# Paged attention on one core: value pages gathered by POOL in four indirect transfers a sequence, in place of sixteen page loads from SP

## What is computed

```
q, k, v   = x Wq, x Wk, x Wv ; q, k normed and rotated        # 32 query heads, 8 key heads, 128 wide
kc, vc    = k_cache[block_table], v_cache[block_table]        # 16 pages of 32 rows: 512 cached keys a sequence
scores    = q . [kc, k] / sqrt(128) ; cached keys past cache_seqlens masked
o         = softmax(scores) @ [vc, v]
out       = x + o Wo
```

## Time and profile before

| | us |
|---|---|
| median of 3 runs | 2616.27 |
| lowest and highest of them | 2610.56, 2620.38 |
| the profiled execution's own time | 2625.55 |
| its span, first to last instruction | 2624.0 |
| PE busy | 2441.7 (93% of the span) |
| DVE busy | 1807.7 (69%) |
| ACT busy | 1592.3 (61%) |
| POOL busy | 428.6 (16%) |

### The profile page before, as it was taken

The page is one execution under the profiler, slowest core; times in us unless marked ns, Lnnn a source line. Parts: engine busy times, 40 slices in busy tenths (PEclk is TensorE's granted clock), DMA queues, the critical chain, the costliest instruction groups (busy, mean ns, idle before and its releaser), DMA issues. The chain is left out here.

```text
span 2624.0 us, 57577 instructions
## 1 busy us (share of the span) xinstructions
PE 2441.7 (93%) x16326; PEld 2210.3 (84%) x16327; DVE 1807.7 (69%) x3636; ACT 1592.3 (61%) x3277; POOL 428.6 (16%) x625
## 2 busy tenths in 40 slices
PE   6699799999999949999999999999999998599999
PEld 5578588877878839999999999999999998388887
DVE  5345336999999948887887778878777785544443
ACT  3122235777777848888888878878788785311111
POOL 1222231010001011222222222222222221000000
PEclk9899899999999979999999999999999999799999
DMA  6422342333333369999999999899999995756664
GB/s 220 148 74 75 124 140 84 97 103 99 100 94 92 89 192 257 294 283 285 290 281 291 282 286 279 276 290 281 279 289 279 275 292 148 275 204 216 219 216 152
DMA packets 388288, 541.09 MB, mean 206 GB/s; under 512 B 61667, under 2 KB 275363, under 8 KB 384356
## 3 DMA queue, kind: packets, MB, share of 16 engines
q1 hardware_dynamic: 352932, 450.10, 56.2%
q0 software_dynamic: 33152, 87.07, 10.2%
q10 hardware_dynamic: 2112, 2.89, 0.4%
HBM read 441.54 MB, written 98.30 MB: 206 GB/s over the span
## 5 line engine op out<-in xcount | busy, mean ns | idle before, releaser
L1514 PE MATMUL att_ps_o<-att_pt,att_v 128*128 128x128 f32 x4096 | 544.2, 276 | 23.0 <-DMA att_v<-in_v_pages 20.8
L1514 PEld LDWEIGHTS att_ps_o<-att_pt,att_v 128*128 128x128 f32 x4096 | 506.0, 192 | 28.5 <-issue 22.2
L1333 ACT ACTIVATE att_prob<-att_prob,att_shift 128x544 f32<-128x544 f32 x512 | 383.7, 749 | 210.0 <-DVE att_shift L1399 196.8
L76 PE MATMUL att_ps_s<-att_k_hi,att_q_hi 128*128 128x272 f32 x1024 | 339.3, 331 | 34.2 <-DVE att_k_lo L1430 22.4
L1399 DVE CUSTOM_DVE_ANT_0 att_prob<-att_ps_s,att_mask 128x544 f32<-128x544 f32 x512 | 366.5, 716 | 0.0
L1430 DVE TENSOR_TENSOR att_k_lo<-att_k_raw,att_k_hi 128x1024 fp32r<-128x1024 f32 (+1 forms) x320 | 338.5, 1058 | 19.6 <-ACT att_k_hi L1348 19.6
L76 PE MATMUL qkv_ps_y<-qkv_w_hi,qkv_xt_hi 128*128 128x512 f32 x768 | 316.2, 412 | 0.0
L1340 ACT ACTIVATE att_pt<-att_ps_pt 128x512 f32<-128x512 f32 x512 | 295.5, 577 | 31.9 <-PE att_ps_pt L1493 30.4
L1493 PE MATMUL att_ps_pt<-att_ident,att_prob 128*128 128x128 f32 x2048 | 309.5, 274 | 1.1 <-ACT att_pt L1340 1.1
L1348 ACT ACTIVATE att_k_hi<-att_k_raw 128x1024 fp32r<-128x1024 f32 (+1 forms) x320 | 292.8, 915 | 28.0 <-DMA att_k_raw<-in_k_pages 28.0
L78 PE MATMUL qkv_ps_y<-qkv_w_hi,qkv_xt_lo 128*128 128x512 f32 x768 | 302.6, 394 | 0.0
(11 more groups left out here) (178 smaller groups left out, 4688.1 us busy)
## 6 DMA issues: line engine op xcount, KB each, us to landing
att_k_raw<-in_k_pages SPq DMA_DIRECT2D x1024, 128.0 KB, 2.9
att_v<-in_v_pages SPq DMA_DIRECT2D x1024, 128.0 KB, 4.3
q_t<-qkv_out_t SPq DMA_DIRECT2D x128, 256.0 KB, 2.3
att_q_raw<-q_t POOLq DMA_DIRECT2D x64, 512.0 KB, 6.6
o_t<-att_o POOLq DMA_DIRECT2D x64, 512.0 KB, 7.4
out_o<-o_t SPq DMA_DIRECT2D x32, 1024.0 KB, 6.2
out_inv<-inv_t SPq DMA_DIRECT2D x32, 1024.0 KB, 6.5
qkv_w_stage<-in_w_qkv SPq DMA_DIRECT2D x12, 1024.0 KB, 5.2
```

Of the source, the lines that this page charges most:

```text
L76: pe.matmul(out, xh, wh, start=start, stop=False)
L1333: act.activation(prob[:, b, :], prob[:, b, :], ACT.Exp, bias=shift[:, b:b + 1], scale=-1.0, accum_out=total[:, j // HK, j % HK:j % HK + 1] ...
L1514: pe.matmul(out, v_sb[:, p, c, h * DH:(h + 1) * DH], pt_sb[:, j % OG, c, :], start=(c == 0), stop=False)
```

## The change

SP loads keys alone. POOL gathers the values: for each sequence four indirect transfers, each of 128 rows of 4 KB, one row into each of the 128 partitions, with row numbers read from SBUF, one a partition. DVE computes the row numbers of all sequences once at the start (`row_sb`: page number times 32 plus the row in the page, from the table, which is now loaded into all 128 partitions, 512 KB, and from `step`, an existing input). For each sequence POOL copies its four columns into `rows_now` between its first and second own-value transfer. POOL's iteration s now loads the own values and the values of s+1, and those of sequence 0 go ahead of the loop; queries and own keys of s+2 and the stores of s-2 stay in iteration s. SP and DVE wait for one count of four small loads; PE waits for 4 landings of values in place of 16. Two pairs of semaphores are merged.

```
-V_ORDER = [c * PPP + m for c in range(NPP // PPP) for m in (0, 2, 1, 3)]
...
+        table_sb, step_sb = m.sb("table", [P, NSEQ * NPP], i32), m.sb("step", [P, 1])
+        row_sb, rows_now = m.sb("row", [P, NSEQ * NPP // PPP], i32), m.sb("rows_now", [P, 2, NPP // PPP], i32)
...
-                def load_v(s, p, pages):
-
-                    if later(s, 2):
-                        sp.wait_ge(pv_done, HK * (s - 1))
-                    for n in V_ORDER:
-                        at = n % PPP * PSIZE
-                        sp.dma_start(v_sb[at:at + PSIZE, p, n // PPP, :], v_pages[bass.ds(pages[n], 1)])\
-                          .then_inc(v_loaded[p], 16)
...
+                sp.dma_start(table_sb[:, :], table).then_inc(small_loaded, 16)
+                sp.wait_ge(small_loaded, 64)
+                load_k(0, 0, pages_in(0))
                 load_k(1, 1, pages_in(1))
 
                 def pair(i, last):
 
                     if not last:
-                        next_pages = pages_in(2 * i + 2)
-                        load_k(2 * i + 2, 0, next_pages)
-                    load_v(2 * i + 1, 1, pages_in(2 * i + 1))
-                    if not last:
-                        load_k(2 * i + 3, 1, pages_in(2 * i + 3))
-                        load_v(2 * i + 2, 0, next_pages)
+                        for p in range(2):
+                            load_k(2 * i + 2 + p, p, pages_in(2 * i + 2 + p))
...
                     for u in range(OG):
+                        if u == 1:
+                            pool.tensor_copy(rows_now[:, p, :], row_sb[:, bass.ds(s * (NPP // PPP), NPP // PPP)])\
+                                .then_inc(rows_copied, 1)
+                            pool.wait_ge(rows_copied, s + 1)
                         pool.dma_start(vo_sb[u * SEQ:(u + 1) * SEQ, p, :, u, :], rows[:, :, u, :])\
                             .then_inc(own_v_loaded[p], 16)
+
+                def load_v(s, p):
+
+                    for c in range(NPP // PPP):
+                        pool.indirect_dma_start(
+                            v_sb[:, p, c, :], None, v_pages.rearrange("n k x -> (n k) x"),
+                            bass.IndirectOffsetOnAxis(ap=rows_now[:, p, c:c + 1], axis=0)).then_inc(v_loaded[p], 16)
...
+                pool.wait_ge(rows_ready, PPP + 2)
+                load_own_v(0, 0)
+                load_v(0, 0)
 
                 def pair(i, last):
+
+
                     for p in range(2):
                         s = 2 * i + p
-                        load_own_v(s, p)
+                        if not (last and p):
+                            load_own_v(s + 1, 1 - p)
+                            load_v(s + 1, 1 - p)
                         if not last:
                             load_q(s + 2, p)
                             load_own_k(s + 2, p)
...
+                row_f = prob[:, 0, 0:NSEQ * NPP // PPP]
+                for m_ in range(PPP):
+                    at = slice(m_ * PSIZE, (m_ + 1) * PSIZE)
+                    dve.tensor_copy(row_f[at, :], table_sb[at, :].rearrange("p (n m) -> p n m", m=PPP)[:, :, m_])\
+                       .then_inc(rows_ready, 1)
+                dve.wait_ge(rows_ready, PPP)
+                dve.tensor_scalar(row_f, row_f, float(PSIZE), step_sb[:, 0:1], ALU.mult, ALU.add).then_inc(rows_ready, 1)
+                dve.wait_ge(rows_ready, PPP + 1)
+                dve.tensor_copy(row_sb[:, :], row_f).then_inc(rows_ready, 1)
...
-                        pe.wait_ge(v_loaded[p], 16 * NPP * (i + 1))
+                        pe.wait_ge(v_loaded[p], 16 * (NPP // PPP) * (i + 1))
...
-        "table": a["itok_Bx16_0_63"].reshape(1, -1),
+        "table": everywhere(a["itok_Bx16_0_63"]),
```

More of the change, by code:

```diff
@@ L1151, with attention @@
 NB_P = OG
-V_ORDER = [c * PPP + m for c in range(NPP // PPP) for m in (0, 2, 1, 3)]
 def pages_of(c):
     return (NPP, 1) if c == PIECE_OWN else ((c if c < PIECE_Q else c - 1) * PPP, PPP)
-def attention(nc, pool_sems, k_pages, v_pages, table, lens, key_at, q_t, k_own, v_own, o_t, inv_t):
+def attention(nc, pool_sems, k_pages, v_pages, table, step, lens, key_at, q_t, k_own, v_own, o_t, inv_t):
     with ExitStack() as ctx:
@@ L1176, in attention @@
         lens_sb, lens_f, key_sb = m.sb("lens", [P, NSEQ], i32), m.sb("lens_f", [P, NSEQ]), m.sb("key_at", [P, NKEY])
-        table_sb = m.sb("table", [1, NSEQ * NPP], i32)
+        table_sb, step_sb = m.sb("table", [P, NSEQ * NPP], i32), m.sb("step", [P, 1])
+        row_sb, rows_now = m.sb("row", [P, NSEQ * NPP // PPP], i32), m.sb("rows_now", [P, 2, NPP // PPP], i32)
         mask = m.sb("mask", [P, 2, NALL])
@@ L1187, in attention @@
         ps_o = m.ps("ps_o", [P, 2, OG, P])
-        zeroed, ident_ready, table_loaded = m.sem("zeroed"), m.sem("ident_ready"), m.sem("table_loaded")
-        small_loaded, lens_ready, mask_ready = m.sem("small_loaded"), m.sem("lens_ready"), m.sem("mask_ready")
+        zeroed, ident_ready = m.sem("zeroed"), m.sem("ident_ready")
+        small_loaded, lens_and_masks = m.sem("small_loaded"), m.sem("lens_and_masks")
         q_loaded, own_k_loaded, own_v_loaded, o_stored, inv_stored = pool_sems
@@ L1193, in attention @@
                     for p in range(2)]
-        v_loaded = m.sems("v_loaded", 2)
+        v_loaded, rows_ready, rows_copied = m.sems("v_loaded", 2), m.sem("rows_ready"), m.sem("rows_copied")
         hi_done, lo_done = m.sem("hi_done"), m.sem("lo_done")
@@ L1226, in _ @@
                 sp.dma_start(key_sb[:, :], key_at).then_inc(small_loaded, 16)
+                sp.dma_start(step_sb[:, :], step).then_inc(small_loaded, 16)
                 def pages_in(s):
                     return nc.values_load_multi_w_load_instructions(
-                        table_sb[:, bass.ds(s * NPP, NPP)], engines=[mybir.EngineType.SP], min_val=0,
+                        table_sb[0:1, bass.ds(s * NPP, NPP)], engines=[mybir.EngineType.SP], min_val=0,
                         max_val=NPAGE - 1, skip_runtime_bounds_check_because="block tables name pages")[1]
@@ L1371, in _ @@
             def _(dve):
-                dve.wait_ge(small_loaded, 32)
-                dve.tensor_copy(lens_f[:, :], lens_sb[:, :]).then_inc(lens_ready, 1)
-                dve.wait_ge(lens_ready, 1)
+                dve.wait_ge(small_loaded, 64)
+                dve.tensor_copy(lens_f[:, :], lens_sb[:, :]).then_inc(lens_and_masks, 1)
+                dve.wait_ge(lens_and_masks, 1)
                 dve.wait_ge(zeroed, 2)
+                row_f = prob[:, 0, 0:NSEQ * NPP // PPP]
[7 more added lines that the diff above has]
+                dve.tensor_copy(row_sb[:, :], row_f).then_inc(rows_ready, 1)
                 def make_mask(s, p):
                     dve.tensor_scalar(mask[:, p, 0:NKEY], key_sb[:, :], lens_f[:, bass.ds(s, 1)], MASKED,
-                                      ALU.is_ge, ALU.mult).then_inc(mask_ready, 1)
-                    dve.wait_ge(mask_ready, s + 1)
+                                      ALU.is_ge, ALU.mult).then_inc(lens_and_masks, 1)
+                    dve.wait_ge(lens_and_masks, s + 2)
                 def wait_for_scores(s, u, j):
@@ L1718, in conditioned_stack @@
         qkv(nc, x3, i["w_qkv"], i["lens_tok"], i["inv_freq"], i["step_pos"], i["norm_w"], q_t, k_own, v_own)
-        attention(nc, pool_sems, i["k_pages"], i["v_pages"], i["table"], i["lens_all"], i["key_at"], q_t,
+        attention(nc, pool_sems, i["k_pages"], i["v_pages"], i["table"], i["step_pos"], i["lens_all"], i["key_at"], q_t,
                   k_own.rearrange("s d c x -> s d (c x)"), v_own, o_t, inv_t)
```

## The result

The changed kernel takes 3201.69 us (median of 4 runs, 3198.07 to 3204.53), the kernel before 2616.54 us beside it: a ratio of 1.2238, with a 95% interval of 1.221 to 1.2266. So it is 585 us slower; the prediction had +425 and a range of 2700 to 3300. The profiled execution has a span of 3203.0 us against 2624.0, 579 more.

What follows compares the result with a forecast made beforehand. PE was taken to set attention's pace, with DMA close behind. A new loop of 24.5 us plus 1.8 for the clock, 26.3 against 19.34 over 61 sequences, gave 2616 + 425 = 3041 us; range 2700 to 3300.

Steps and rivals of the forecast that it cites:

- The loop: Attention: inverse store now meets its reciprocal, closing a POOL-DVE-PE loop of X + 8.5 us; it sets the period above 18.78.
- X: Time from POOL's start to the landing of the inverse store: 16.0 us, bounds 13.7 to 22.4, harmless up to 10.3.
- the prediction's second way: X without queue order: issues of POOL's transfers up to the inverses 8.9 us, plus the store's median landing 7.0: 15.9.
- the first way: X by bytes in POOL's queue: 3.7 us to the first gather, 3.81 MB at 369 GB/s 10.3, start-up and receipt 2.0.
- The clock: PE in attention: a 5.7 us gap each sequence drops the granted clock, adding 1.8 us, for a period of 26.3.
- The sum: Attention turns: 61 x (26.3 - 19.34) = +425 us, with the 34 us of late values included.
- Edits at nothing: Own keys, queries, output store, SP's lighter list, PE's fewer counts, value landings and DVE's row numbers: no cost.
- The start: Start of attention: 512 KB table delays first loads, but sequence 1's keys skip 2 MB of values: 0, between -10 and +8.
- The rule against the change: POOL's gathers: skill page's 3100 ns issue beside two-port DVE work would make four take 12.4 us, period about 8 longer.
- Rival 1: Attention: values on time and nothing else, X under 10.3, period 18.78: -34 us, 2582; chance 0.04.
- Rival 2: Attention: gathers run in their own queue and delay nothing, period 20 to 21.4: +40 to +126 us; chance 0.08.
- Rival 3: Attention: dear gathers, issue 2.4 us each, X 19 to 21.5: +608 to +760 us, 3224 to 3376; chance 0.14.

Runs made afterwards that it cites:

- the gap filled: Changed kernel with 56 extra discarded PE products a sequence just ahead of PE's wait for the reciprocal: 3103.70 us, ratio 1.1867.
- the first experiment: Changed kernel with the same gathers, but POOL's iteration s loads own values and values of s again, not s+1: 2595.66 us, ratio 0.9916.
- the last kernel: Changed kernel with POOL's iteration not shifted, and SP loading 16 table partitions before the first keys, the rest after: 2584.96 us, ratio 0.9888.
- the shift alone: Kernel before, values still loaded by SP, with POOL's own values and so its iteration one sequence ahead, no gathers: 2878.34 us, ratio 1.1006.

## Where the prediction was right and where it was wrong

**The loop: right.** Releaser by releaser it is as told: inverses to DVE, DVE to PE, PE to POOL, 61 times. The runs bear out its form at four values of X: 10.87 (turn 19.67), 13.53 (23.39), 17.79 with the gap filled (26.84) and 17.82 (28.58); and with the shift undone the turn is 18.77, the undisturbed 18.78 of the earlier trace rows. At full clock X + 8.5 holds: the rest of the turn is 8.51 and 8.52 in the median in the two kernels that kept the clock (8.80 and 9.05 in the mean; the second still stands in some turns).

**X: 16.0 forecast, 17.8 measured; this is the term that was mis-sized.** By the prediction's second way (issue, then landing) the issue of the inverses is at 9.99 and not 8.9, and the landing takes 7.8 in the median and not 7.0. Within the issue: own values, with the copy and its wait, 3.26 us instead of 2.7 (the copy 0.22, but the wait behind it 0.71); four gathers 5.10 instead of 4.0, since 0.30 us of idle time come with each, and its 0.97 of issue were nearly the 1.0 taken; queries, own keys and outputs 1.63 instead of 2.18. By the first way (bytes): 14 us at 311 GB/s are 4.35 MB instead of 3.81. That fits two of SP's key pieces in this turn (3.28 + 2 x 0.52) where one was taken, and the mean rate was under the 369 taken: while the gathers were still being issued, the two stretches of 2 us from 1819 on moved 231 and 276 GB/s. So each way fell short by its own small terms. The bounds of X, 13.7 to 22.4, held it.

**The clock: 1.8 forecast, about 2 measured.** By the turn's rest it is 10.75 - 8.5 = 2.2, by the filled gap 1.74. The row it was taken from the earlier trace rows was a gap of 3.56 us; the gaps here are about 7.6 (464.0 / 61). Those rows show the slow stretch behind one of the three waits alone; the trace of the kernel before has a granted clock of 0.50 behind the other two as well (1724 to 1726 and 2076 to 2078 us).

**The sum.** 61 x (28.58 - 26.3) = 139 us are missing in the turns. Two more pieces are small: POOL's first start is 5.15 us later (1015.16 against 1010.01), where the prediction took 0 between -10 and +8 for the start, and behind POOL's last start the span goes on for 444.7 us against 434.4, 10 us more, where the sum counted 61 turns and nothing behind them: the last reciprocal of attention comes 5.5 us later after that start, and the rest falls into the start of the output projection. 139 + 5 + 10 = 154, and 425 + 154 = 579, the difference of the profiled spans.

**Edits at nothing: held.** No wait for values in any stretch, no cost of DVE's row numbers (six operations, where the prediction counts seven), none of SP's lighter list. The cover was named rightly: own keys at unit 0 came next when the inverses went earlier.

**The start: the balance was wrong.** The 512 KB table took 7.4 us to land and put the first key pages at 959.07, 7 us after before's 952.07. What the prediction set against it did come (first scores at 977.35, where they had been at 966.12, but PE's next wait 1.56 us where 11.72 stood). A wait of 4.04 us for ACT's probabilities was new, and about 5 us were left over.

**The rule against the change: a hold shows, but it is rare here.** The prediction argued from plain transfers (0.53 to 0.56 us in rows 3, where it says 0.54 to 0.57) and said that no row shows a gather. Gathers took 933 to 1558 ns to issue, 966 in the median, with DVE busy 54% of the stage; in the first experiment, with DVE busy 82%, the median is 967 and the longest of 256 is 1948. The 3100 ns that the Trainium skill gives (SBUF — State Buffer, "A bandwidth-pool intuition that's wrong (but worth ruling out)") for a POOL transfer beside a DVE copy are not reached in these traces; the longest gather of any run takes 2409, with the gathers last. But POOL does wait for DVE: the nine gathers of the changed kernel that took over 1100 ns all began while DVE was in its two-input operation, and none of the other 247 took more than 1042. With the gathers last, 64 began in one, 60 of them took over 1100 ns, and the median end is 0.81 us behind the end of DVE's operation. One of them, in the kernel with the gathers last:

```profile
1515.31 1.34 POOL L1289 DMA_INDIRECT att_v<-in_v_pages,att_rows_now  x1 [0.30 <-issue]
```

```profile
1514.62 1.22 DVE L1447 TENSOR_TENSOR att_k_lo<-att_k_raw,att_k_hi 128x1024 fp32r<-128x1024 f32 x1
```

Plain transfers that began in such an operation took at most 630 ns in the changed kernel (284 of them), so the prediction's reading holds for these alone. Why gathers and the copy of row numbers are held and plain transfers are not was not tested.

**The rivals.** Rival 1's price, -34 us, is what the gathers are worth without the loop: its turn of 18.78 is met in the first experiment, where the loop's shift was taken out, and the last kernel has -31 us. It did not come because X was 17.8 and not under 10.3. Rival 2 fell: the gathers stand ahead of the inverses. Rival 3's range (3224 to 3376) begins just above the measured time, but its reason did not come: the issue is 0.97 and not 2.4, and a hold by DVE met only nine of the 256 gathers.

**Left open.** A second buffer for the inverses, which would cut the loop with the shift kept, was not tried, nor was issuing the stores from another engine. Why 0.30 us pass ahead of each gather was not settled.

## What to carry to other kernels

When a load is moved one step ahead in an in-order queue, list everything else that the same loop body issues: the waits of the first instruction move the stores behind it too, and a store that was a turn ahead of its reader can come to meet it. Work out the loop so made (start, issue, bytes ahead, landing, back to the start) and compare it with the turn; small stores that free a buffer belong ahead of large loads that are wanted a turn later. Then add the clock: a gap that returns each turn cost the gap and 1.7 to 2.2 us more here. And see what DVE does when POOL issues its gathers: beside a two-input operation they take longer.

## What was not expected of the hardware

- An indirect gather of 128 rows of 4 KB takes POOL 0.97 us and 0.30 us of idle time ahead of it, 1.27 in all, against 0.56 for a plain transfer of 128 rows. A copy of 128x4 numbers takes 0.22 us, but what waits for it on POOL itself goes on 0.71 us later.
- POOL's gathers and its small copy from SBUF wait for DVE's two-input fp32 operation (1.2 us for 128x1024) if they begin in it: a gather then ends 0.81 us behind it in the median, the copy 0.04 us. Plain transfers go on.
- With four gathers over 128 partitions the stage keeps the DMA engines less busy than with sixteen pages of 32 partitions for the same data: 0.87 at 291 GB/s in the first experiment against 0.94 at 283.
- A 4 KB store lands 7.8 us after its issue (median) in the changed kernel, with megabytes ahead of it in its own queue, and 8.6 in the shift alone, with 1.1 MB there and SP's value pages beside it; its least in the changed kernel is 2.6.
- Here idle PE cost more than its idle time, and useless work gave that back: 56 discarded products a sequence made the kernel 98 us faster.
